# Four engines' programs reordered at the start and at two layer boundaries of a four-layer graph network kernel

## The reference

```
layer 0: w = (q * (adj @ k)).sum(-1) / sqrt(512);  L = softmax(w)[:, :, None] * (h @ Wv)     (q, k = halves of h @ Wqk)
layer 1: W = adj * exp(q @ k.T), rows divided by their sums;  L = W @ v       (q, k, v = h @ W.T + b)
layer 2: 8 heads of 64: L = (softmax(q @ k.T / 8 * (adj + adj)) @ v) @ Wo.T + bo
layer 3: T = adj * exp(leaky_relu(si[:, None] + sj[None, :] + ab)), rows divided by their sums
         (sj, si: dots of h @ Wv + bv with the halves of aw)
         L = relu(h @ Wk[0] + T h @ Wk[1] + T T h @ Wk[2] + sum of bk)
```

## Time and profile before

| | |
|---|---|
| median of three runs | 2256.65 us |
| profiled execution | 2256.77 us |
| its span, first to last instruction | 2255.0 us |
| mean granted TensorE clock | 0.996 |
| TensorE busy | 2225.3 us, 99% |
| VectorE / ScalarE / GpSimd busy | 58% / 35% / 32% |
| chain that ended last | TensorE 92% |
| DMA | 220.53 MB, mean 98 GB/s |

### The profile page before, as it was taken

One profiled execution on the slowest core, in us unless ns is written; L12 is line 12 of the kernel. 1 busy time (PEld: TensorE's weight loads), 2 busy tenths in 40 slices (PEclk: granted clock), 3 DMA queues, 4 the chain that ended last, 5 costly groups with the idle time before them and its releaser, 6 DMA issues.

```text
span 2255.0 us, 39107 instructions
## 1 busy us (share of the span) xinstructions
PE 2225.3 (99%) x15788; PEld 1764.4 (78%) x15788; DVE 1299.4 (58%) x2615; ACT 781.8 (35%) x1393; POOL 714.9 (32%) x923
## 2 busy tenths in 40 slices
PE   8999999999999999999999999999899999999999
PEld 5788888887888777888888888888777777777776
DVE  3565555655555576455656455656566757575742
ACT  3423333333323343333232333333433444444442
POOL 1433433334333423223332223332341323232320
PEclk9999999999999999999999999999999999999999
DMA  6333333333333344332333332333443333333331
GB/s 209 75 79 104 91 101 82 89 92 86 88 93 99 90 134 121 110 85 81 89 108 85 105 95 81 88 99 93 135 130 96 94 94 102 100 89 111 84 92 38
DMA packets 150935, 220.53 MB, mean 98 GB/s; under 512 B 42849, under 2 KB 48993, under 8 KB 150753
## 3 DMA queue, kind: packets, MB, share of 16 engines
q1 hardware_dynamic: 144608, 209.62, 32.7%
q10 hardware_dynamic: 6144, 8.40, 1.5%
HBM read 84.71 MB, written 50.37 MB: 60 GB/s over the span
## 4 chain that ended last, share of the span: by engine, by line
PE 92%; SPq 2%; DVE 2%; DMA 2%; issue 1%; ACT 1%; POOL 1%; DVEq 0%; ACTq 0%
PE bank L317 52%; PE bank L307 29%; PE bank L333 3%; PE bank L570 3%; SPq L961 2%; PE bank L505 2%; PE bank L475 1%; PE bank L368 1%; PE bank L297 1%; DVE hs L647 1%; ACT g1T L1017 0%; DMA hGA<-hs 0%; DMA si<-stB 0%; DVE yt L943 0%; PE bank L556 0%
## 5 line engine op out<-in xcount | busy, mean ns | idle before, releaser
L317 PE MATMUL bank<-w_hi,h3T_hi 128*128 128x512 f32 x768 | 306.1, 399 | 2.3 <-POOL w_lo L1216 2.3
L317 PE MATMUL bank<-w_lo,h3T_hi 128*128 128x512 f32 x768 | 300.0, 391 | 0.0
L317 PE MATMUL bank<-w_hi,h3T_lo 128*128 128x512 f32 x768 | 299.8, 390 | 0.0
L968 ACT ACTIVATE Z<-bank 64x512 f32<-64x512 f32 x256 | 151.7, 593 | 220.8 <-PE bank L317 203.6
L982 ACT ACTIVATE hn<-x,stA 128x512 f32<-128x512 f32 x192 | 140.7, 805 | 183.2 <-POOL stA L1226 183.2
L317 PEld LDWEIGHTS bank<-w_hi,h3T_hi 128*128 128x128 f32 x768 | 144.5, 188 | 58.0 <-issue 25.2
L622 DVE BATCH_NORM_STATS2 stA<-x 128x6 f32<-128x512 f32 x192 | 128.3, 668 | 86.1 <-DMA x<-mid 76.5
L1221 POOL TENSOR_SCALAR stA<-stA 128x4 f32<-128x4 f32 x48 | 11.5, 239 | 507.7 <-DVE stA L624 507.5
L317 PEld LDWEIGHTS bank<-w_hi,h3T_lo 128*128 128x128 f32 x768 | 144.5, 188 | 30.5
L317 PEld LDWEIGHTS bank<-w_lo,h3T_hi 128*128 128x128 f32 x768 | 144.6, 188 | 29.1
L1234 POOL TENSOR_TENSOR h1T_lo<-hGB,h1T_hi 128x512 fp32r<-128x512 f32 x64 | 80.7, 1290 | 202.8 <-ACT h1T_hi L968 202.8
(11 more groups left out here) (197 smaller groups left out, 5702.8 us busy)
## 6 DMA issues: line engine op xcount, KB each, us to landing
hGA<-hs SPq DMA_DIRECT2D x760, 64.0 KB, 2.0
mid<-x SPq DMA_DIRECT2D x32, 1024.0 KB, 4.5
x<-mid SPq DMA_DIRECT2D x32, 1024.0 KB, 5.9
x<-in_x SPq DMA_DIRECT2D x16, 1024.0 KB, 5.8
hGB<-hs SPq DMA_DIRECT2D x256, 64.0 KB, 2.0
out<-x SPq DMA_DIRECT2D x15, 1024.0 KB, 6.4
PT<-hs SPq DMA_DIRECT2D x120, 64.0 KB, 2.1
PT<-hs ACTq DMA_DIRECT2D x120, 64.0 KB, 2.1
```

Source lines behind the costliest of these rows:

```text
L317: ins = eng.matmul(b[:], h[l][:, k, ts], W[r][:, k, :], start=(k == 0 and i == 0), stop=(last and k == 3 and i == 2))
L968: return eng.activation(dst, src, ACT.Copy)
```

## The change

No operation is added to or removed from the kernel, and TensorE's program is the same instruction for instruction. What changes is the place of operations in the programs of the other four engines, and for one of them the engine.

1. **Start.** x of group 0 is loaded behind the first two slices of Wqk. The adjacency block, the masks and Wv0 are loaded before Wk1 and Wq1, and SyncE's half of the first gather comes behind all weights of layers 0 and 1. The lo parts of group 0's features are made by GpSimd instead of VectorE.
2. **Layer 1 to 2.** VectorE makes q2w_lo behind vf of group 14 instead of before it, and h2T_lo of group 0 behind the x update of group 14; transposes(2, 1) come behind k2w_lo instead of before it. ScalarE makes q2w_hi one pass later, SyncE loads x of group 1 for layer 2 behind the store of group 14.
3. **Layer 2 to 3.** In pass 15, statistics, normalisation, transposes and gather of layer 3's group 0 and its hi parts come later; SyncE writes `arows` before that gather. In pass 16 VectorE computes all dots of group 0 before the lo parts of the second half of ctx(15). In layer 3's pass 0 ScalarE makes exp and hi parts of group 1 before its Z copies, as in all other passes, and GpSimd's `l3_alpha(1)` stands before `features_lo(3, 1)`.

VectorE (`dve_program`):

```diff
             split_W(Wm0, "m0")
-            features0_lo()
...
             for g in range(NG + 1):
                 on0, on1, on_pv = g < NG, g >= 1, g >= 2
+                if g == NG:
+                    split_in_place(Wq2, "q2")
                 if on_pv:
                     l01_x2(g - 2)
...
-                    if g == NG - 1:
-                        split_in_place(Wq2, "q2")
-                        features2_lo(0)
                 else:
+                    features2_lo(0)
                     stats_A(2, 1)
+                    split_in_place(Wk2, "k2")
                     transposes(2, 1)
-                    split_in_place(Wk2, "k2")
...
-                if g == NG - 1:
-                    stats_A(3, 0)
                 if prev:
                     l2_ctx(g - 1, 0)
...
                 if g == NG - 1:
-                    transposes(3, 0)
                     dve.wait_ge(d_vec3, 64)
...
                 if g == NG:
+                    l3_sums(dve, eng, 0, (0, 1))
                     l2_out(g - 2, 3)
-                    l3_sums(dve, eng, 0, (1,))
+                    l3_sums(dve, eng, 0, (2, 3))
+                    l2_out(g - 1, 0)
                     l2_ctx(g - 1, 1)
-                    l2_out(g - 1, 0)
-                    l3_sums(dve, eng, 0, (2, 3))
                     stats_A(3, 1)
...
-                if 0 < g < NG - 1:
+                if g:
                     stats_A(*after2(g))
...
                     l2_ctx(g - 1, 1)
+                if g == NG - 1:
+                    transposes(3, 0)
...
-                if g == NG - 1:
-                    l3_sums(dve, eng, 0, (0,))
```

ScalarE (`act_program`):

```diff
                 else:
+                    split_in_place(Wq2, d_q2)
                     act.wait_ge(*bank.done(("v1", NG - 2, 3)))
...
-                    if g == NG - 1:
-                        split_in_place(Wq2, d_q2)
...
-                if g == NG - 1:
-                    norm_A(3, 0)
                 if on:
                     l2_evict("k2", g, KK, 4, a_k)
...
                 if g == NG - 1:
-                    act.wait_ge(v_cst, 1)
-                    act.wait_ge(*bank.done(("v2", NG - 2, 3)))
-                    features2_hi(3, 0, hT3[0])
+                    norm_A(3, 0)
...
+                    act.wait_ge(v_cst, 1)
+                    features2_hi(3, 0, hT3[0])
...
-                if g == 0:
-                    act.wait_ge(*bank.done(("v2", NG - 1, 3)))
-                    features2_hi(3, 1, hT3[1])
                 l3_T_other(g)
                 if g + 2 < NG:
                     norm_A(3, g + 2)
-                if g == 0:
-                    for t in range(4):
-                        l3_z(1, ("z1", 0, t), 0, t)
-                    l3_exp(1)
-                    continue
                 if g + 1 < NG:
                     l3_exp(g + 1)
-                    act.wait_ge(*bank.done(("y", g - 1, 3)))
+                    act.wait_ge(*bank.done(("y", g - 1, 3) if g else ("v2", NG - 1, 3)))
                     features2_hi(3, g + 1, hT3[(g + 1) % 2])
```

GpSimd (`pool_program`), where the two additions into `bsum` also move ahead of layer 3's loop:

```diff
             l01_am(0)
+            features_lo(0, 0, hT[0], hGA, p_flo0)
             split_in_place(Wv0, "v0")
...
-                if g == 0:
-                    features_lo(3, 1, hT3[1], hGA, p_flo3)
-                    l3_alpha(1)
...
-                elif g + 1 < NG:
+                if g + 1 < NG:
                     l3_alpha(g + 1)
                     features_lo(3, g + 1, hT3[(g + 1) % 2], hGA, p_flo3)
```

SyncE (`sp_program`):

```diff
-            load_x(0, x_v[0])
             for k in range(4):
+                if k == 2:
+                    load_x(0, x_v[0])
                 eng.dma_start(qT[:, k, :], qk_rows[:, k, :]).then_inc(d_qk[k], 16)
...
-            eng.dma_start(wk1[:], rows(L1_gnn_Wk_w)).then_inc(d_k1, 16)
-            gather(0, 0, (0, 1))
-            eng.dma_start(wq1[:], rows(L1_gnn_Wq_w)).then_inc(d_q1, 16)
             load_adj(0)
             load_mask(0)
             eng.dma_start(Wv0["raw"][:], rows(L0_gnn_Wv)).then_inc(d_v0, 16)
+            eng.dma_start(wk1[:], rows(L1_gnn_Wk_w)).then_inc(d_k1, 16)
+            eng.dma_start(wq1[:], rows(L1_gnn_Wq_w)).then_inc(d_q1, 16)
...
+            gather(0, 0, (0, 1))
...
-                else:
-                    load2(g + 1 - NG)
+                elif g + 1 == NG:
+                    load2(0)
...
+            load2(1)
             gather(2, 1)
...
-                    gather(3, 0)
                     sp.wait_ge(v_af, 8)
...
-                if 0 < g < NG - 1:
+                if on and g:
                     gather(*after2(g))
```

More of the change, by code:

```diff
@@ L648, in transposes @@
                                   (hn1 if layer == 1 else hn)[t][:].rearrange("p (c b r) -> p c b r", c=4, b=4)).then_inc(v_tr, 1)
[L650 to L653, removed]
             def features2_lo(g):
@@ L1342, in pool_program @@
             split_in_place(W3[0], "w0")
+            pool.wait_ge(d_bk3, 16)
+            eng.tensor_tensor(bsum[:], bkb[:, 0, :], bkb[:, 1, :], ALU.add).then_inc(p_bsum, 1)
+            pool.wait_ge(p_bsum, 1)
+            eng.tensor_tensor(bsum[:], bsum[:], bkb[:, 2, :], ALU.add).then_inc(p_bsum, 1)
             for g in range(NG):
@@ L1347, in pool_program @@
                     scale_A(3, g + 2)
-                if g == 0:
-                    features_lo(3, 1, hT3[1], hGA, p_flo3)
-                    l3_alpha(1)
-                    pool.wait_ge(d_bk3, 16)
-                    eng.tensor_tensor(bsum[:], bkb[:, 0, :], bkb[:, 1, :], ALU.add).then_inc(p_bsum, 1)
-                    pool.wait_ge(p_bsum, 1)
-                    eng.tensor_tensor(bsum[:], bsum[:], bkb[:, 2, :], ALU.add).then_inc(p_bsum, 1)
-                elif g + 1 < NG:
+                if g + 1 < NG:
                     l3_alpha(g + 1)
```

## The result

The changed kernel takes 2290.34 us (median; 2287.05 to 2293.01) against 2256.60: **1.0149, 95% interval 1.0132 to 1.0167**, slower by 33.7 us. The forecast was 2281.1 (2268 to 2290): right in sign and in the largest place, too small by 9.2 us and outside its range by 0.3. The profiled execution took 2293.74 (span 2291.9), 37.0 more than that of before, and is the slowest of the five, so its sum is some 3 us above the median's.

The account below looks back on a forecast made before the run. TensorE's work plus some 30 us of stops was taken to bound the kernel. Start +2.5, layer 1 to 2 +25.1 and layer 2 to 3 -3.3 made +24.3 on 2256.77: 2281.1 us, range 2274 to 2287, or 2268 to 2290 with rivals.

Parts of the forecast that it names:

- Layer 1 to 2: TensorE stops 13.2 us for h2T_lo, then 8.9 in k2 for a bank the x update frees; with clock +25.1.
- the clock's 2 x 1.5: Time lost to TensorE's lower clock after the two new stops between layers 1 and 2, 1.5 us each.
- Line 475: Layer 3's scores: earlier arows writes cut TensorE's 5.8 us stop to 1.8, with no clock fall: -4.0-1.7.
- o2 for cT_lo: Ahead of ctx(15)'s second lo parts VectorE makes eight dots and two adds; TensorE waits: +4.1, and 1.5 of clock.
- Before y: Earlier dots bring w0_lo sooner, so TensorE no longer waits there and 1.9 us of clock returns: -4.6.
- The hop: Layer 3's first pass: ScalarE's Z copies wait behind group 1's exp and h3T_hi; TensorE stands 1.4 us.
- layer 2 to 3: All steps between layers 2 and 3 together: a gain, -3.3 us, bounds -8 and +4.
- The start: Late gather and GpSimd's lo parts put g0 at about 35.0: +1.0 and 1.5 of clock, +2.5; upper bound +4.5.
- Rival 2: Layer 3's gain fails, the 5.8 us stop stays, early dots cost +4, start at upper bound: 2290; chance 0.12.

Follow-up runs that it names:

- c1_arows_first: Kernel before, with only SyncE's 4-byte arows writes issued ahead of layer 3's first gather: 2253.24 us, 0.9987.
- after_add_first: Changed kernel with VectorE's fourth residual add of group 14 moved ahead of the first eight dots in layer 2's last pass: 2287.98 us, 1.0133.
- c_only: Kernel before with only the change's edits between layers 2 and 3: 2262.80 us, 1.0025.
- c_hop_only: Kernel before with only layer 3's first-pass order on ScalarE and GpSimd changed (group 1's exp ahead of h3T_hi and Z copies, bsum before the loop): 2265.82 us, 1.0022.
- a_only: Kernel before with only the start changed (SyncE's first load order, group 0's lo parts on GpSimd): 2261.90 us, 1.0021.

## Why the prediction was wrong

- **Layer 1 to 2: right in mechanism.** Both stops and their releasers came, of 12.7 us for 13.2 and 7.5 for 8.9. Of the clock's 2 x 1.5 there, 1.65 and 2.5 or more were measured. That the sum is right to 0.1 us is luck: the dearer clock made up what the stops fell short.
- **Line 475: right.** The stop was 2.4 (1.8 forecast) without half clock, and that the writes cause it is shown. That a stop of 1.8 is "too short for a fall of the clock" no run shows: the clock stayed at 1.00 behind this one's 0.9 + 1.5, but fell behind c1_arows_first's 2.1. after_add_first, with the same writes, stood 4.5 us here.
- **o2 for cT_lo:** the stop was exact (4.1); its clock cost 3.2, not 1.5.
- **Before y:** w_lo's wait fell to 0.7 and the clock came back, -4.0 for -4.6. In c_only it did not fall (2.3), so it rests on how late the rest is.
- **The hop, the step that failed:** "ready at 1684.2, TensorE at 1682.8: 1.4", with no clock after it. The changed kernel lost 5.8 us there, a stop of 4.0 and 1.8 of clock. With cT_lo's clock this makes layer 2 to 3 a loss and not the gain of 3.3. c_hop_only has the clear case: TensorE was there at 1683.6, the exp at 1682.7, the first two copies of Z1 at 1686.4, stop 2.8 and 1.7 of clock that the step left out. In the changed kernel VectorE's late add held SyncE's store and with it si, and the stop was 4.0. Nor did the forecast have anything for the rest of layer 3, where the changed kernel lost 2.5 us and c_hop_only 2.7; since such waits also come without a change there, this part is not shown to be the hop's.
- **The start, mis-sized:** it cost +6.0 in this execution and +4.1 in a_only's, where the forecast was +2.5 and its bound +4.5. x was seen at 10.96, not 9.2, and the gather's first quarter at 32.40, not 29.0. The bytes ahead were counted rightly; the rate was not. The bound was worked out wrongly, too: the same sum at its 0.31 MB/us gives g0 at 38.2, not 37, and so +5.7 with clock, not +4.5; g0 began at 38.10. The changed kernel moved, in 40 slices of the first 50 us:

```profile
GB/s 0 116 341 338 182 336 360 400 381 278 263 345 383 390 385 388 383 390 387 313 188 213 251 197 177 274 371 244 272 341 139 26 13 0 0 0 0 0 0 0
```

From 25.0 to 32.5 us, where the gather's pieces run, it has 177 to 274 GB/s and not the 350 that I took from the earlier trace rows; 7.5 us at some 217 are 2.8 us of the 3.4. Small packets are not the reason: the gather's move 2048 bytes each, as most of the weights' do. Why this stretch is slower is not shown. Half of Wqk and x, 2.1 MB, were seen when 3.0 MB had moved, since the other half ran along with them.

In all, the miss of 12.7 us in the profiled execution is 5.5 of clock (+7.9 measured; the terms had 1.5 + 3.0 - 1.7 + 1.5 - 1.9 = 2.4) and 7.2 of stops: 3.1 before g0, 2.6 for Z, some 2 later in layer 3 and 0.7 for PT, less 1.7 in layer 1 to 2, and 0.5 in small ones.

Rival 2's number came (2290 for 2290.34) without its condition: it needed a stop at line 475 of 5.8 us, and that was 2.4. This agreement is luck.

## What to carry to other kernels

Price the clock after a new stop from the worst row, not the mildest: the changed kernel lost from 1.65 to 2.5 us in the first 5 us behind stops of 4 to 13 us, and the longest stop was not the dearest. Ask of each operation moved ahead on an in-order engine whether its input is a round trip through DRAM (the exp here: si written, read, alpha): behind it everything waits. And a DMA of 1024 4-byte pieces can stop an engine that never waits for it; gather the pieces on chip first.

## What the runs showed of the hardware

- 1024 4-byte pieces from SBUF to DRAM took 10.9 us from issue to the end of the wait, the same bytes in 128 pieces 2.4, and TensorE stood 5.8 us or not at all. In fourteen kernels with the 4-byte pieces it stood 2.4 to 6.6 us in all, in the three with larger pieces not at all.
- A start with 7.9 MB queued ahead moved 64 KB gather pieces in 7.0 us (median), where they took 2.0 before.
- q2w_lo, two tiles in SBUF, took 5.71 beside GpSimd's h1T_lo, k2w_lo 2.50 alone, which agrees with the rule of the Trainium skill named in the prediction (SBUF — State Buffer, Who interferes with whom); v2w_lo took 4.63, beside GpSimd's adds for 3.6 us of it.
